# Context scores of a head pair made together on the two halves of PE's rows, in the score banks

## The reference, cut to what matters

```python
x = layer_norm(x, ln1_w, ln1_b)               # here: the context, 77 tokens
lat = layer_norm(latents, ln2_w, ln2_b)       # here: the 512 tokens of x
lat = lat * (1.0 + scale[:, None, :]) + shift[:, None, :]
q = einsum('bld,ed->ble', lat, Wq)
kv_in = concatenate((x, lat), axis=-2)        # 77 + 512 keys
kv = einsum('bld,ed->ble', kv_in, Wkv)
k, v = split(kv, 2, axis=-1)
logits = einsum('bhqd,bhkd->bhqk', q * attn_scale, k * attn_scale)
w = softmax(logits, axis=-1)
out = einsum('bhqk,bhkd->bhqd', w, v)
return einsum('ble,de->bld', out, Wo)
```

## Time and profile before

| | |
|---|---|
| median of 3 runs | 2709.22 us |
| profiled execution | 2708.3 us |
| its span | 2706.2 us |
| PE busy | 2496.4 us (92%) |
| DVE busy | 2056.4 us (76%) |
| ACT busy | 1842.0 us (68%) |
| POOL busy | 1079.0 us (40%) |
| mean granted clock of PE | 0.955 |

### The profile page before, as it was taken

How to read it: one execution, slowest core, us unless ns; L and a number is a source line. 1 busy time by engine, 2 the same in 40 slices (tenths; PEclk the granted TensorE clock), 3 DMA queues, 4 the chain that set the end, 5 groups by cost and what they waited for, 6 DMA issues and landing times.

```text
span 2706.2 us, 45204 instructions
## 1 busy us (share of the span) xinstructions
PE 2496.4 (92%) x16138; PEld 1098.0 (41%) x16138; DVE 2056.4 (76%) x4367; ACT 1842.0 (68%) x3703; POOL 1079.0 (40%) x1342
## 2 busy tenths in 40 slices
PE   7999899998977899999999999999999999999677
PEld 3545454554532233333333333333333333333334
DVE  5776958868677788888888888888888888875322
ACT  3665657656524587877777778787777887777532
POOL 2544535445533344444343344433344444432311
PEclk9999999999957899999999999999999999999878
DMA  2000000000031222222212122212121222220000
GB/s 74 1 1 1 1 1 1 1 26 1 26 70 38 60 55 72 58 63 55 72 48 61 53 68 56 64 48 66 48 58 50 70 55 65 56 66 22 20 10 8
DMA packets 108569, 113.01 MB, mean 42 GB/s; under 512 B 15809, under 2 KB 96951, under 8 KB 107319
## 3 DMA queue, kind: packets, MB, share of 16 engines
q1 hardware_dynamic: 108345, 110.12, 14.9%
HBM read 14.80 MB, written 1.05 MB: 6 GB/s over the span
## 4 chain that ended last, share of the span: by engine, by line
PE 58%; DVE 22%; POOL 7%; issue 4%; ACT 3%; DMA 3%; SPq 3%; DVEq 0%; POOLq 0%; ACTq 0%
PE psum L1114 8%; DVE A L1585 7%; PE psum L1097 6%; PE psum L913 5%; PE psum L1085 4%; DVE A L1607 4%; PE psum L1206 4%; PE psum L1020 4%; PE psum L986 4%; PE psum L1213 3%; PE psum L995 3%; SPq L810 2%; PE psum L1178 2%; PE psum L974 2%; PE psum L1273 2%
## 5 line engine op out<-in xcount | busy, mean ns | idle before, releaser
L1585 DVE TENSOR_REDUCE A<-psum 128x1 f32<-128x512 f32 x1536 | 1006.5, 685 | 193.3 <-PE psum L1097 182.6
L1802 ACT ACTIVATE A<-psum 128x512 f32<-128x512 f32 x1536 | 821.6, 601 | 149.1 <-PE psum L1114 79.2
L1097 PE MATMUL psum<-A 64*128 64x512 bf16 x1536 | 476.7, 392 | 25.8 <-DVE A L1585 18.0
L1085 PE MATMUL psum<-A 64*128 64x512 bf16 x1536 | 413.0, 387 | 16.4 <-ACT A L1802 8.0
L1114 PE MATMUL psum<-A 128*32 128x512 f32 x3072 | 414.2, 612 | 1.0 <-ACT A L1811 0.2
L1946 POOL TENSOR_TENSOR A<-A,rden 128x512 f32<-128x512 f32 x256 | 265.3, 1058 | 246.1 <-DVE rden L1472 246.1
L1097 PEld LDWEIGHTS psum<-A 64*128 64x128 bf16 x1536 | 120.2, 95 | 452.9 <-DVE A L1585 399.4
L1832 ACT ACTIVATE A<-psum 77x512 f32<-77x512 f32 x384 | 206.9, 593 | 50.7 <-PE psum L1169 49.6
L913 PE MATMUL psum<-ident,A 128*128 128x128 f32 x1264 | 201.8, 286 | 41.1 <-DVE A L1332 14.1
L1977 POOL TENSOR_TENSOR A<-A 128x512 f32<-128x512 f32 (+1 forms) x78 | 96.8, 1241 | 321.6 <-DMA A<-A 321.6
L1743 ACT ACTIVATE A<-psum,nm 128x512 f32<-128x512 f32 x256 | 175.4, 685 | 61.7 <-DVE nm L1458 61.3
(11 more groups left out here) (211 smaller groups left out, 4138.9 us busy)
## 6 DMA issues: line engine op xcount, KB each, us to landing
A<-A SPq DMA_DIRECT2D x456, 128.0 KB, 2.4
A<-A SPq DMA_DIRECT2D x336, 64.0 KB, 2.0
A<-zero SPq DMA_DIRECT2D x51, 128.0 KB, 2.3
wl<-in_wl SPq DMA_DIRECT2D x6, 1024.0 KB, 6.2
A<-A SPq DMA_DIRECT2D x36, 78.0 KB, 2.1
A<-in_nT SPq DMA_DIRECT2D x1, 1664.0 KB, 7.1
A<-in_w SPq DMA_DIRECT2D x2, 512.0 KB, 7.1
A<-in_w SPq DMA_DIRECT2D x1, 1024.0 KB, 6.5
```

What stands on the lines that cost most here:

```text
L1085: handle.matmul(bank(b), k_st[bt][lo:lo + ROW, h // 2, k * P:(k + 1) * P], q_st[m % 3][lo:lo + ROW, h // 2, :], start=True, stop=True).the ...
L1097: handle.matmul(bank(b), q_st[m % 3][lo:lo + ROW, pair, q * P:(q + 1) * P], k_st[bt][lo:lo + ROW, pair, :], start=True, stop=True).then_in ...
L1585: handle.tensor_reduce(nm[:, pair // 4, q, j, pair % 4:pair % 4 + 1], bank(3 + j), AX.X, ALU.max, negate=True).then_inc(mx, 1)
L1802: handle.activation(pT[:, block % 2, i % GROUP, :], bank(ring_of["scores", m, i]), ACT.Exp, scale=HD1 ** -0.5).then_inc(ex, 1)
```

## The change

The context's scores are one piece per pair instead of one per head. The four blocks of queries are the outer loop and the two heads the inner one, so that products on partitions 0 to 63 and 64 to 127 alternate; the heads go to two banks, b and b+1. These are two of banks 0 to 3: the function score_banks gives each pair of heads five turns on the two pairs of banks, the first for the context's scores and four for the blocks of queries. ctx_max copies and reduces both heads in one instruction each. TENSOR0 has 208 pieces instead of 216, VECTOR0 131 instead of 139. All four tables of the first layer have new places. Bank 4 no longer holds context scores.

```diff
+        def score_banks(u, q):
+            return 2 * ((5 * u + q + 1) % 2)
...
         TENSOR0 = {
-            "ctx_scores": [-35, -30, 6, 16, 31, 40, 56, 60, 85, 88, 109, 112, 134, 137, 161, 165],
-            "scores": [-29, -22, -17, -9, 17, 20, 25, 27, 41, 44, 48, 55, 61, 62, 74, 86, 87, 93, 97, 101, 113, 114, 125, 128, 135, 138,
-                146, 152, 162, 166, 180, 185],
+            "scores": [2, 3, 12, 13, 35, 41, 46, 50, 57, 58, 67, 72, 82, 85, 91, 100, 107, 108, 114, 118, 133, 140, 143, 149, 157, 161,
+                167, 172, 180, 181, 191, 197],
+            "ctx_scores": [-1, 34, 54, 78, 103, 132, 155, 176],
...
         VECTOR0 = {
-            "ctx_max": [-47, -42, -26, -21, -11, -5, 4, 7, 23, 25, 40, 44, 59, 62, 80, 83],
+            "ctx_max": [-120, -102, -89, -74, -60, -40, -25, -7],
...
                 if name == "ctx_scores":
-                    u, j = divmod(i, 2)
-                    lo = j * HD0
-                    pe.wait_ge(pqa, NP0 * bt + u + 1)
-                    pe.wait_ge(pca, NP0 * bt + u + 1)
-                    free(4)
+                    b = score_banks(i, -1)
+                    pe.wait_ge(pqa, NP0 * bt + i + 1)
+                    pe.wait_ge(pca, NP0 * bt + i + 1)
+                    free(b)
+                    free(b + 1)
                     for q in range(QT):
-                        t = handle.matmul(psum[:, 4, q * P:q * P + C], q_pair[lo:lo + HD0, u % 2, q * P:(q + 1) * P],
-                                          k_pair[lo:lo + HD0, u % 2, S:KV], start=True, stop=True)
-                    t.then_inc(cs, 1)
-                    owner[4] = (cs_m, 2 * NP0 * bt + i + 1)
+                        for j in range(2):
+                            lo = j * HD0
+                            t = handle.matmul(psum[:, b + j, q * P:q * P + C], q_pair[lo:lo + HD0, i % 2, q * P:(q + 1) * P],
+                                              k_pair[lo:lo + HD0, i % 2, S:KV], start=True, stop=True)
+                            if q == QT - 1:
+                                t.then_inc(cs, 1)
+                    owner[b] = owner[b + 1] = (cs_m, NP0 * bt + i + 1)
                 if name == "scores":
-                        b, lo = 2 * (i % 2) + j, j * HD0
+                        b, lo = score_banks(u, q) + j, j * HD0
...
                 if name == "ctx_max":
-                    u, j = divmod(i, 2)
-                    g = NP0 * bt + u
-                    src = four(bank(4))[:, :, 0:C]
-                    dve.wait_ge(cs, 2 * NP0 * bt + i + 1)
+                    g, b = NP0 * bt + i, score_banks(i, -1)
+                    src = psum[:, b:b + 2, :].rearrange("p j (q t) -> p j q t", q=QT)[:, :, :, 0:C]
+                    dve.wait_ge(cs, 2 * g + 2)
                     if g:
                         dve.wait_ge(xc, 2 * QT * (g - 1))
-                    handle.tensor_copy(c_sc[:, u % 2, j, :, :], src)
-                    handle.tensor_reduce(nmc[:, u % 2, j, :], src, AX.X, ALU.max, negate=True).then_inc(cs_m, 1)
+                    handle.tensor_copy(c_sc[:, i % 2, :, :, :], src)
+                    handle.tensor_reduce(nmc[:, i % 2, :, :], src, AX.X, ALU.max, negate=True).then_inc(cs_m, 1)
                 if name == "maximum":
-                    gi, s, r = UNITS * bt + i, 2 * (i % 2), i % 4
+                    gi, s, r = UNITS * bt + i, score_banks(u, q), i % 4
-                    dve.wait_ge(cs_m, 2 * NP0 * bt + 2 * u + 2)
+                    dve.wait_ge(cs_m, NP0 * bt + u + 1)
...
-                    handle.activation(p0[r][:, j, :], bank(2 * (i % 2) + j), ACT.Exp, bias=nm0[:, r, j:j + 1],
+                    handle.activation(p0[r][:, j, :], bank(score_banks(u, q) + j), ACT.Exp, bias=nm0[:, r, j:j + 1],
```

More of the change, by code:

```diff
@@ L335, in build @@
         TENSOR0 = {
[L336 to L341, removed]
@@ L348, in build @@
[L348 to L355, removed]
+                        "turn": [20, 32, 33, 37, 38, 40, 43, 44, 51, 53, 56, 60, 61, 64, 66, 68, 73, 74, 77, 79, 80, 83, 86, 87, 97, 98, 105, 106,
+                109, 111, 112, 116, 120, 122, 123, 125, 130, 131, 138, 141, 147, 151, 152, 158, 159, 162, 164, 169, 170, 173, 179, 188, 189, 192,
@@ new lines, in build @@
+                199, 201, 208, 209, 215, 217, 222, 223, 225, 226],
+                        "scores": [2, 3, 12, 13, 35, 41, 46, 50, 57, 58, 67, 72, 82, 85, 91, 100, 107, 108, 114, 118, 133, 140, 143, 149, 157, 161,
+                167, 172, 180, 181, 191, 197],
+                        "weigh": [47, 48, 55, 63, 69, 76, 88, 93, 94, 95, 102, 104, 113, 115, 119, 126, 127, 128, 134, 135, 145, 146, 154, 156, 165,
+                182, 183, 184, 205, 206, 212, 213, 214, 218, 219, 229, 230, 231, 232, 233],
@@ new lines, in build @@
+            "project_q": [-21, 8, 42, 52, 96, 110, 148, 168],
+            "ctx_turn": [36, 39, 62, 65, 90, 92, 121, 124, 142, 144, 163, 166, 190, 194, 224, 227],
+            "project_k": [-8, 26, 45, 59, 99, 117, 150, 171],
+            "out": [235, 236, 237, 238],
+            "project_c": [-5, 31, 49, 75, 101, 129, 153, 174],
+            "ctx_scores": [-1, 34, 54, 78, 103, 132, 155, 176],
+            "b_turn": 278,
+            "b_up": [279, 289, 292, 297],
+            "b_turn2": [344, 345],
@@ L361, in build @@
[L361 to L367, removed]
@@ new lines, in build @@
+            "q_out": [4, 29, 47, 58, 94, 108, 134, 149],
+                        "turned": [41, 43, 45, 49, 59, 63, 66, 69, 77, 80, 83, 85, 99, 102, 106, 110, 116, 119, 122, 129, 140, 141, 147, 150, 155,
+                165, 168, 175, 181, 186, 189, 191],
+            "ctx_turned": [42, 44, 64, 70, 88, 90, 115, 118, 128, 131, 144, 146, 166, 169, 190, 194],
+            "k_out": [15, 37, 50, 61, 96, 112, 136, 152],
+            "c_out": [18, 40, 54, 76, 98, 121, 137, 154],
+            "weighed": [72, 93, 114, 125, 158, 179, 187, 195],
@@ L375, in build @@
+            "b_scale": 219,
+            "b_turned": 230,
+            "b_relu": [232, 240, 241, 246],
+            "b_square": 248,
+            "b_scale2": 262,
+            "b_turned2": [282, 283],
         }
         VECTOR0 = {
-                        "maximum": [-41, -38, -35, -32, -20, -18, -15, -13, -4, -2, 0, 3, 9, 11, 16, 24, 26, 29, 33, 36, 46, 49, 53, 56, 63, 66, 69,
-                72, 84, 86, 91, 95],
-                        "turned": [-29, -27, -25, -22, -12, -9, -6, -3, 1, 6, 10, 12, 17, 21, 27, 32, 35, 37, 42, 52, 55, 65, 68, 71, 73, 78, 85,
@@ L391, in build @@
[L391 to L406, removed]
+            "ctx_kv": -131,
@@ new lines, in build @@
+            "v_out": [-139, -130, -127, -125, -121],
+                        "turned": [-107, -103, -100, -97, -91, -87, -84, -82, -77, -75, -72, -69, -62, -59, -56, -54, -48, -45, -43, -38, -31, -26,
+                -21, -19, -12, -4, 2, 8, 14, 17, 19, 20],
+                        "maximum": [-119, -116, -113, -109, -101, -98, -95, -92, -86, -85, -80, -78, -71, -70, -67, -63, -57, -55, -52, -49, -39,
+                -36, -33, -29, -23, -20, -16, -11, -5, -2, 3, 7],
+                        "divide": [-115, -110, -108, -106, -96, -93, -90, -88, -81, -79, -76, -73, -68, -64, -61, -58, -53, -50, -47, -41, -35, -32,
+                -27, -24, -18, -14, -10, -6, -1, 5, 9, 13],
@@ new lines, in build @@
+            "ctx_max": [-120, -102, -89, -74, -60, -40, -25, -7],
+            "x_out": 26,
+            "b_stats": 27,
+            "b_norm": 32,
+            "b_square": 37,
+            "b_quant": 48,
+            "b_affine": 65,
+            "b_square2": 66,
+            "b_max": 80,
+            "b_levels": 85,
+            "b_round": 87,
+            "b_clip": 89,
+            "b_out": 94,
+            "lat_norm": -165,
+            "lat_stats2": -161,
+            "lat_norm2": -159,
+            "lat_kv": -153,
@@ L407, in build @@
+            "x_norm": 245,
+            "x_stats": 116,
+            "lat_stats": -275,
+            "ctx_norm": -140,
+            "ctx_stats": -265,
         }
         POOL0 = {
[L409 to L412, removed]
@@ L419, in build @@
+            "lat_power": 408,
+            "ctx_power": 409,
+            "lat_power2": 417,
+            "x_power": 662,
+            "b_power": [531, 536, 553],
         }
```

42 lines of the change are left out of this document (13 added, 29 removed).

## The result

The changed kernel takes 2668.62 us (median of 4 runs, 2667.10 to 2671.32), the kernel before 2710.2 beside it: ratio 0.9855, 95% interval 0.9843 to 0.9867. It is 41.6 us faster. The forecast was 2686, so 24 us, with a range from 2668 to 2711. The direction was right and 18 us of the gain were not foreseen. The time lies 0.6 us inside the low edge of the range, and outside what each of the four theories of the prediction gave for itself (A: 2674 to 2699).

What follows compares the result with a forecast made beforehand. PE's work in order was taken to bound the first layer, the only part changed. Terms 27 + 3 - 4 - 3 = 23 us took the profiled 2708.3 to 2685.3, plus 0.9 for the median: 2686 us, range 2668 to 2711.

Steps and rivals of the forecast that it cites:

- A: Whole kernel: the gain comes as forecast, 2674 to 2699 us; chance 0.63.
- PE's order sets the time in the first layer: First layer: PE's work in order sets the time, except for DVE's full stretches and PE's handoff waits.
- 0.88 us for the pair, loads of two halves side by side: Context's scores on PE: loads of two row halves overlap, so a pair costs 0.88 us, as one head did.
- Rival C: Context's scores on PE: the halves don't overlap, PE saves nothing and pays eight more runs; 2707 to 2711 us, chance 0.10.
- the lower end of 0.54: Context's scores on PE: lowest pair cost, eight steps at the pace of their columns alone, 0.54 us.
- (16 - 8) x 0.88 for the pairing: PE per batch: eight fewer head costs, less 2 x 0.16 for added runs, save 6.7 us; 27 in four batches.
- Bank 4's handoff, 4.4 us: PE's waits before the context's scores, ended by DVE's reduction, go: 4.4 us, of which 3 were counted as gain.
- The fifth turn of the banks: Scores' banks, first layer: an added turn per pair brings two new waits, for exponentials and context reduction; 4 us lost.
- Rival D: Scores' banks: the added turn chains PE to DVE's copy and reduction, so the kernel is slower, 2724 us; chance 0.12.
- DVE's full stretches, 3 us lost: Feed-forward laid over the next attention, three batches: DVE is full, so PE's saving counts less; 3 x 1.1 = 3 us lost.
- New places, counted as nothing, between +8 and -8: First layer's orders: same work interleaved much alike, so no effect counted, between +8 and -8 us.
- The clock, rival B: First layer: DVE's stretches and more PE work at half clock absorb most of the gain, leaving 9 us, 2700; chance 0.15.

Runs made afterwards that it cites:

- pair_twice: Changed kernel with every pair's context scores made twice in the same banks, adding PE work only; 2691.35 us, 22.7 above the changed kernel.
- old_places_eased: New pieces in the earlier kernel's orders, with score units (4, 0) and (4, 1) moved four and three pieces later on PE; 2736.44 us, ratio 1.0107.
- new_serial: Changed kernel with only the loops over heads and query blocks swapped, so heads run one after the other; 2684.05 us, ratio 0.9905.
- old_places: Changed kernel's pieces in the orders of the kernel before, merged context pieces at one of their two earlier places; 2730.65 us, ratio 1.0074.

## Why the forecast was right in direction and short in size

- **PE's order sets the time in the first layer**: right, at 0.8 us of time per microsecond added to the context's scores (pair_twice), not 1.
- **0.88 us for the pair, loads of two halves side by side**: right. By the forecast's own count the pair takes 0.89. Rival C and the lower end of 0.54 are out. The Trainium skill (TensorE: Matmul & The Clock Gate, on the 56 ns gap) gives some 62 ns per matmul where the sequencer decodes it, 0.99 us for sixteen. That does not bind here: 0.95 from start to next start is already under it.
- **(16 - 8) x 0.88 for the pairing**: right as a sum. PE has 32.5 us less work up to the fourth products, where 27 were forecast. As a cause it is wrong: half of what the line saves comes with one piece in place of two, the loops alone give 15 to 18 us, and with the old orders the new pieces save PE 14.0 us of work and the time still grows.
- **Bank 4's handoff, 4.4 us**: gone as forecast (0.4 left before L980). I counted 3. Bank 4's projections wait 1.4 us more.
- **The fifth turn of the banks**: I named two new waits and missed the third, that (u, 0) now follows the exponentials of (u-1, 3). In the new order it costs little; PE's waits before scores are 1.0 us for ACT's L1749 and 0.7 for the reduction, not the 4 us that I counted. In the old order it shows as 29.6 us. Rival D had the fifth turn as the danger, but by way of the reduction; the wait that grew is the one for the exponentials. That it is this wait which the new places avoid at a gain is not shown: old_places_eased took 11.6 us of it away and was no faster.
- **DVE's full stretches, 3 us lost**: the stretches are still there, earlier in time as all of the batch is. This is one of 25 us after, to set against the earlier trace rows; DVE has 23.74 and PE 20.74. What it costs can't be read from the trace.

```profile
260.00:285.00 25.00, 20.74 (x108) 10.09 (x110) 23.74 (x40) 17.98 (x47) 19.04 (x16) 0.93 0.00 1
```

- **New places, counted as nothing, between +8 and -8**: this is the step that failed. At fixed new pieces, the new orders are worth 2730.65 - 2668.6 = 62 us; at the old pieces they cost 68. I argued from the likeness of the two orders piece by piece. What the runs show is that pieces and orders cannot be priced one by one. I take it that what counts is whether each bank's last reader is done when PE comes to it; this is argued from the waits, and no run isolates it.
- **The clock, rival B**: the profile's mean clock did not fall, it is 0.959 where it was 0.955. Of batches 2 and 3 it was 0.97 and 0.96 and is 0.97 and 0.98. As an estimate from these means, 8% of the third batch at 1.2 instead of 2.4 GHz became 4%: 14.7 us became 6.8, worth about 4 us. That agrees with the larger gain of the third batch but was not tested by itself, and the means are rounded to 1%.

Two slips in the prediction's numbers: 744.2 is the end of the fourth output products and not their start, which was 737.15 (they now start at 697.3 and end at 704.7, where I expected about 720). And 11 us below 2686 is 2675; the low end of 2668 is reached only with the 8 us of the places on top.

That the direction came out right is in part luck. The forecast gave all of its 23 us to the pieces, with nothing for the orders; with the old orders these pieces are 20 us slower than before. And that 2668.6 is inside the range owes to a low end taken from a pair of 0.54 us, which did not happen. In PE's account the forecast is 17 us short like this: 5.5 us more work saved than the 27, and idle time that fell by 7.4 where the terms +3 - 4 - 3 let it rise by 4. The clock may be part of the first. In the second, PE's waits before the turns fell by 11.2 us and other waits grew. How the orders bring this about was only read from the traces.

## What to carry to other kernels

Where engines run fixed orders tied through shared banks, list for each changed bank who must be done before its next writer, and the work between; do it for every reader, not only for the operations that changed. That check would have found the wait that the forecast missed. An order is made for its pieces: here each half of the change alone lost 20 to 70 us, and together they won 42. So price a change of pieces and a change of orders together, and run the two apart before giving either the credit. A tiny instruction on the path (a join of two maxima, 0.16 us at its shortest) deserves a look at its longest instance, not its median: rewriting it won 17 us more, and 12 to 14 in the kernel before.

## What the runs showed of the hardware that was not expected

- Two groups of fp32 products on different row halves, issued one after the other, overlap by themselves: 1.55 us for sixteen where 1.92 was expected from 0.88 a head (new_serial). Alternating them gave 1.05.
- A DVE instruction with two SBUF inputs that begins while POOL runs a product of two tensors lasts until that product ends: 0.16 us at its shortest, and 2.86, 2.94 and 4.48 us behind one of 4.5 us that began 1.7, 1.6 and 0.03 us earlier. With one tensor input and a scalar operand it stayed at 0.202 to 0.216 in 256 instances.
- Behind 7.5 us in which PE was all but idle the granted clock is 0.50, and a unit of scores takes 2.99 us in place of 1.1 (old_places).
